# A two-stage vision block on one core: two roots to GpSimd as a power, 64x64 identity matmuls for the transposes, contiguous evictions, a new order with six early expert units

## The reference

```
x: (4, 64, 64, 16) fp32
x = x + conv_block(ln_over_channels(x))
t = tokens(x);  t = t + moe(ln(t));  x = from_tokens(t)

conv_block: x_dct = DCT over both axes
  low : 8x8 windows; q, k, v = window @ W; q, k normalised over the 64 places;
        attention over 16x16 channels per head; proj, bias
  high: h1 = gelu(1x1 conv); h1 = gelu(3x3 depthwise); x_conv = h1 + x_dct;
        h2 = gelu(1x1 conv of x_conv);  high = h2 + x_conv
  out = inverse DCT of (coef * low + (1 - coef) * high + x_dct)
moe: 8 experts 64 -> 256 -> 64 with exact gelu, all computed; the two largest
     router weights of a token gate the sum
```

## Time and profile before

| | us |
|---|---|
| Median of 3 runs (228.62 to 231.86) | 231.08 |
| The profiled execution | 230.22 |
| Its span, first to last instruction | 228.0 |
| PE busy | 199.9 (88%) |
| DVE busy | 131.4 (58%) |
| ACT busy | 127.3 (56%) |
| POOL busy | 51.9 (23%) |
| DMA, mean rate over the span | 63 GB/s |
| Mean granted TensorE clock | 0.978 |

### The profile page before, as it was taken

The page is one execution under the profiler, slowest core; times in us unless marked ns, Lnnn a source line. Parts: engine busy times, 40 slices in busy tenths (PEclk is TensorE's granted clock), DMA queues, the critical chain, the costliest instruction groups (busy, mean ns, idle before and its releaser), DMA issues.

```text
span 228.0 us, 6079 instructions
## 1 busy us (share of the span) xinstructions
PE 199.9 (88%) x2674; PEld 105.6 (46%) x2674; DVE 131.4 (58%) x231; ACT 127.3 (56%) x207; POOL 51.9 (23%) x54
## 2 busy tenths in 40 slices
PE   6868797999928977839689999999999999999992
PEld 2544486773404557737134344444444444444430
DVE  0597047909996998699981633554333554334554
ACT  2337942230072955546967587666687666786630
POOL 5380096019109996030120000000000000000000
PEclk9979999999997999997999999999999999999999
DMA  6990000000000000000004954360805406062001
GB/s 203 282 267 12 0 6 3 4 3 3 0 0 3 1 3 3 3 3 6 0 0 150 228 116 88 73 157 3 184 0 125 108 19 167 3 157 73 3 0 46
DMA packets 6601, 14.27 MB, mean 63 GB/s; under 512 B 2736, under 2 KB 4144, under 8 KB 5680
## 3 DMA queue, kind: packets, MB, share of 16 engines
q1 hardware_dynamic: 6576, 13.89, 24.8%
HBM read 12.71 MB, written 1.18 MB: 61 GB/s over the span
## 4 chain that ended last, share of the span: by engine, by line
PE 58%; DVE 26%; ACT 6%; DMA 5%; issue 3%; SPq 1%; DVEq 0%
PE psum L730 22%; PE psum L712 20%; PE psum L555 3%; DMA wide<-gate_store 2%; DMA xs<-in_x 2%; PE psum L529 2%; DVE place L1063 2%; PE psum L565 1%; PE psum L515 1%; DVE row L1062 1%; DVE place L1059 1%; DVE place L1007 1%; DVE place L1112 1%; DVE st L1106 1%; DVE st L1003 1%
## 5 line engine op out<-in xcount | busy, mean ns | idle before, releaser
L712 PE MATMUL psum<-tok,w1s 128*64 128x512 f16 x512 | 60.3, 382 | 2.0 <-ACT w1f L881 1.2
L1186 DVE SCALAR_TENSOR_TENSOR term<-psum,sm,wide 128x512 f32<-128x512 f32 x32 | 24.0, 751 | 59.1 <-PE psum L730 51.6
L881 ACT ACTIVATE hid<-psum,b1p 128x512 f32<-128x512 f32 x64 | 38.2, 700 | 15.5 <-PE psum L712 15.2
L712 PEld LDWEIGHTS psum<-tok,w1s 128*64 128x64 f16 x512 | 28.8, 111 | 35.5 <-issue 8.9
L730 PE MATMUL psum<-hid,w 128*64 128x512 f32 x128 | 28.9, 593 | 0.0
L881 ACT ACTIVATE w1f<-psum,b1p 128x512 f32<-128x512 f32 x32 | 19.5, 687 | 15.5 <-PE psum L712 15.4
L1191 DVE TENSOR_TENSOR x<-x,term 128x512 f32<-128x512 f32 x32 | 22.1, 692 | 1.1
L881 ACT ACTIVATE w1g<-psum,b1p 128x512 f32<-128x512 f32 x32 | 19.6, 712 | 0.3 <-PE psum L712 0.3
L730 PEld LDWEIGHTS psum<-hid,w 128*64 128x64 f32 x128 | 9.1, 137 | 15.0 <-issue 9.7
L555 PE MATMUL psum<-h_pad,tap_bd 64*64 64x512 f32 x144 | 16.0, 590 | 0.0
L730 PE MATMUL psum<-w1g,w 128*64 128x512 f32 x64 | 15.1, 594 | 0.1
(11 more groups left out here) (147 smaller groups left out, 289.9 us busy)
## 6 DMA issues: line engine op xcount, KB each, us to landing
wide<-gate_store SPq DMA_DIRECT2D x14, 512.0 KB, 6.3
xs<-in_x SPq DMA_DIRECT2D x2, 512.0 KB, 4.6
w1f<-in_W SPq DMA_DIRECT2D x2, 512.0 KB, 9.2
block_out<-x SPq DMA_DIRECT2D x4, 256.0 KB, 6.5
wide<-gate_store SPq DMA_DIRECT2D x2, 384.0 KB, 5.0
hid<-in_W1T SPq DMA_DIRECT2D x1, 512.0 KB, 10.2
w<-in_W SPq DMA_DIRECT2D x1, 512.0 KB, 12.3
sm<-in_small SPq DMA_DIRECT2D x1, 407.0 KB, 6.6
```

What stands on the lines that cost most here:

```text
L712: mm = pe.matmul(h_bank(tile)[side * H:(side + 1) * H, :], w1s[:, part, e, k * P + side * H:k * P + (side + 1) * H], tok[:, pair, half, b, :],
L881: act.activation(hid_of[u % 4][:, B2 * k + b, :], h_bank(tile), ACT.Gelu, bias=b1p[:, e * KT + k:e * KT + k + 1]).then_inc(gelu_ready, 1)
L1186: dve.scalar_tensor_tensor(term[:, u % 2, :], y_bank(u), b2t[:, e:e + 1], gate_b[part][:, e % (E // 2), :], ALU.add, ALU.mult).then_inc(te ...
```

## The change

- **Roots.** `inverse_root` stays for the column norms. For the norms of q and k and for the token variances, POOL does one `tensor_tensor` with the operation power and a tensor of -0.5 (new stages `root_of_norms`, `root_of_tokens`). DVE's stages are cut in two at that place (`inverse_norms` | `spread_roots`, `norm_tokens` | `scale_tokens`), with other work between.
- **Transposes.** `windows`, `places`, `heads` and `to_frequencies` become 32 matmuls of 64x64 blocks with a 64x64 identity each instead of 8 full transposes. Each has one semaphore increment at its end instead of one for each half.
- **Layout.** Copies from PSUM read and write in order (the output of `keep_dw` in runs of 8). The strides go into matmuls: `dct_over_w` and `windows` write PSUM with a step of 8 elements, `to_frequencies` loads weights with a step of 8, `inverse_over_kh` with a step of 16. `mix_branches` and `residual` lose their strides, the gates are made by one instruction instead of two, and the store of the gates writes 64-element runs.
- **Order.** All of `TURN` is new. Six units have an early `up` and two an early `down` and add. POOL makes the experts' weights (`weights_of_first`) after the first root.
- `SHARED` would give some of the copies to DVE; it is zero everywhere, so ACT does all of them.

```
 TURN = {
-    "router_weights": (1, 4), "keep_router_weights": (1, 4), "weights_of_first": (1, 2), "dct_over_h": (2, 3),
+    "root_of_norms": (1, 4), "root_of_tokens": (10, 12), "spread_roots": (9, 17), "scale_tokens": (30, 35),
+    "router_weights": (1, 4), "keep_router_weights": (3, 4), "weights_of_first": (2, 13), "dct_over_h": (2, 3),
...
-EARLY, EARLY_DOWN = 4, 0
-UPS = (45, 47, 48, 49, 50, 51, 52, 55)
-DOWNS = ()
-GELUS = (33, 34, 35, 36, 38, 39, 42, 44)
-ADDS = ()
+EARLY, EARLY_DOWN = 6, 2
+UPS = (45, 47, 48, 49, 50, 52, 54, 56, 58, 59, 60, 62)
+DOWNS = (53, 55)
+GELUS = (34, 35, 36, 37, 38, 40, 43, 44, 45, 46, 47, 50)
+ADDS = (39, 41)
...
-                    mm = pe.matmul(slot(p, 1)[rows_of(b), by_half(cp, side)], dh[p][rows_of(side), by_half(cp, b)], dct_w[rows_of(side)],
-                                   start=True, stop=True)
+                    to = bank(slot(p, 1), side).rearrange("p (m c) -> p c m", c=CP)[rows_of(b), cp]
+                    mm = pe.matmul(to, dh[p][rows_of(side), by_half(cp, b)], dct_w[rows_of(side)], start=True, stop=True)
...
-                for k2 in range(K):
-                    mm = pe.transpose(slot(p, 0)[:, k2 * P:(k2 + 1) * P], dw[p][:, k2 * P:(k2 + 1) * P], ident)
-                    if k2 % 4 == 3:
-                        mm.then_inc(xd_done, 1)
+                for k2, side, b in quarters():
+                    mm = pe.matmul(phase(slot(p, 0), b, k2)[rows_of(side)],
+                                      dw[p][rows_of(b), by_side(k2, side)], half_ident[rows_of(b)], start=True, stop=True)
+                mm.then_inc(xd_done, 1)
...
+                for k2, b, side in quarters():
+                    mm = pe.matmul(bank(slot(p, 1), side)[rows_of(b), k2 * H:(k2 + 1) * H],
+                                      phase(x_out[p], b, k2)[rows_of(side)], half_ident[rows_of(side)], start=True, stop=True)
+                mm.then_inc(back_done, 1)
...
+                of_channel = back[p].rearrange("p (m c) -> p c m", c=C)
...
-                    act.wait_ge(xd_done, 2 * p + j + 1)
-                    act.copy(xd[p].rearrange("p (n k) -> p k n", k=K)[:, 4 * j:4 * j + 4],
-                             bank(slot(p, 0), j).rearrange("p (k n) -> p k n", n=P)).then_inc(xd_ready, 1)
+                act.wait_ge(xd_done, p + 1)
+                for j in banks("xd", p):
+                    act.copy(bank(xd[p], j), bank(slot(p, 0), j)).then_inc(xd_ready, 1)
...
+            def root_of_norms(p):
+                pool.wait_ge(norms_read, p + 1)
+                r = root[:, p]
+                pool.tensor_tensor(r[:, 1, :], r[:, 3, :], minus_half[:, :], ALU.pow).then_inc(norm_roots, 1)
+
+            def root_of_tokens(p):
+                pool.wait_ge(vars_ready, p + 1)
+                two = lambda a: st[:, p, a:a + 2, :].rearrange("p a g -> p (a g)")
+                pool.tensor_tensor(two(4), two(2), minus_half[:, 0:2 * G], ALU.pow).then_inc(token_roots, 1)
```

More of the change, by code:

```diff
@@ L43 @@
 TURN = {
-    "router_weights": (1, 4), "keep_router_weights": (1, 4), "weights_of_first": (1, 2), "dct_over_h": (2, 3),
-    "square_columns": (2, 3), "dct_over_w": (5, 7), "windows": (6, 9), "conv_in": (8, 11), "keep_dw": (5, 7),
-    "keep_xd": (6, 9), "gelu_in": (8, 11), "norm_columns": (1, 2), "places": (10, 13), "keep_xt": (10, 12),
-    "join": (3, 5), "rest_ahead": (4, 7), "high": (6, 8), "gram_matrices": (12, 15), "gram_times_w": (14, 17),
-    "norms": (16, 20), "mask_gram": (5, 7), "taps": (19, 22), "logits": (18, 23), "products": (6, 9),
@@ L49 @@
-    "keep_tk": (13, 14), "inverse_norms": (8, 11), "scale_logits": (10, 14), "norms_of_k": (21, 25),
-    "softmax_in": (12, 15), "softmax_out": (13, 17), "gelu_depthwise": (15, 17), "gelu_out": (18, 22),
-    "conv_out": (24, 29), "project": (26, 31), "exponent": (16, 21), "heads": (27, 32), "times_wv": (28, 33),
-    "keep_y": (19, 23), "low": (30, 35), "mask_mix": (16, 19), "keep_yt": (20, 24), "to_frequencies": (34, 38),
-    "inverse_over_kh": (36, 41), "keep_back": (25, 27), "keep_half": (26, 29), "square_tokens": (28, 32),
@@ new lines @@
+    "square_columns": (1, 2), "dct_over_w": (5, 8), "windows": (6, 10), "conv_in": (7, 12), "keep_dw": (5, 8),
+    "keep_xd": (6, 10), "gelu_in": (7, 11), "norm_columns": (1, 2), "places": (9, 14), "keep_xt": (9, 13),
+    "join": (3, 6), "rest_ahead": (5, 8), "high": (7, 9), "gram_matrices": (11, 16), "gram_times_w": (13, 18),
+    "norms": (15, 20), "mask_gram": (4, 7), "taps": (19, 22), "logits": (17, 23), "products": (5, 8),
+    "keep_tk": (12, 14), "inverse_norms": (6, 11), "scale_logits": (12, 19), "norms_of_k": (21, 25),
@@ new lines @@
+    "softmax_in": (13, 20), "softmax_out": (14, 22), "gelu_depthwise": (15, 17), "gelu_out": (19, 22),
+    "conv_out": (26, 27), "project": (24, 30), "exponent": (16, 20), "heads": (28, 32), "times_wv": (29, 33),
+    "keep_y": (18, 23), "low": (31, 35), "mask_mix": (23, 25), "keep_yt": (21, 24), "to_frequencies": (34, 38),
+    "inverse_over_kh": (36, 40), "keep_back": (25, 27), "keep_half": (26, 29), "square_tokens": (28, 32),
+    "mix_branches": (24, 27), "inverse_over_kw": (37, 42), "high_part": (30, 42), "tokens": (39, 44),
@@ L114, in constants @@
     out[:, CONST["dct_h"]] = twice(centred.T)
-    out[:, CONST["dct_w"]] = twice(dct.T)
+    by_phase = np.arange(W).reshape(2, WW // 2, K).transpose(0, 2, 1).reshape(-1)
+    out[:, CONST["dct_w"]] = twice(dct.T[:, by_phase])
     out[:, CONST["idct_h"]] = twice(idct.T)
-    out[:, CONST["idct_w"]] = twice(idct.T)
+    out[:, CONST["idct_w"]] = twice(idct.T[by_phase])
     out[:, CONST["ident"]] = np.eye(P)
@@ L344, in metaformer @@
         norms_read = sem("norms_read")
+        norm_roots, vars_ready, token_roots = (sem(n) for n in ("norm_roots", "vars_ready", "token_roots"))
+        dw_other, xd_other, xt_other, yt_other, back_other, half_other = (
+            sem(f"{n}_other") for n in ("dw", "xd", "xt", "yt", "back", "half"))
         (sq_ready, dh_ready, dw_ready, xd_ready, h1_ready, halo_ready, xt_ready, gram_ready, prod_ready, tk_ready,
@@ L961, in weights_of_first @@
                 pool.tensor_tensor(w1s[:, 1, :, :], w1g[:, :, :], w1s[:, 0, :, :], ALU.subtract).then_inc(w1_ready, 1)
-            for stage, (p,) in in_turn((weights_of_first, join, rest_ahead, high, low_part)):
+            for stage, (p,) in in_turn((weights_of_first, join, rest_ahead, high, low_part, root_of_norms, root_of_tokens)):
                 stage(p)
@@ L1151, in shares @@
                 link(dve.scalar_tensor_tensor(L[5], L[5], 0.5, over(s[:, 14, :], E), ALU.mult, ALU.mult))
-                for half in range(2):
-                    part = lambda a: a[:, half * K:(half + 1) * K].rearrange("p (t b) e -> p b e t", b=B2)
-                    total = dve.scalar_tensor_tensor(gates[:, p, half], part(L[2]), 0.5, part(L[5]), ALU.mult, ALU.add)
-                total.then_inc(gparts_ready, 1)
+                by_row = lambda a: a.rearrange("p (t b) e -> p (b e) t", b=B2)
+                dve.scalar_tensor_tensor(gates[:, p].rearrange("p b e t -> p (b e) t"), by_row(L[2]), 0.5, by_row(L[5]),
+                                         ALU.mult, ALU.add).then_inc(gparts_ready, 1)
             def biases(p):
```

165 lines of the change are left out of this document (98 added, 67 removed).

## The result

The changed kernel takes 264.39 us (median of 3 runs, 264.13 to 264.93) against 231.08 us before: 1.148 times the time, 95% interval 1.137 to 1.159. It is 33.3 us slower, where 222.0 us was forecast. The profiled execution has a span of 262.6 us and a mean granted clock of 0.903 (before 228.0 and 0.978).

The account below looks back on a forecast made before the run. PE was taken to bound the rounds, no engine to be full in the front. Rounds begin at 119.3, plus 96.3 and 4.25 behind: 219.8 us span against 228.0, minus 8.2, so 222.0 us; range 216 to 230.

Parts of the forecast that it names:

- The price of the power: POOL's power for the roots: 3.1 us for 128x128, 0.8 for 128x32 with hand-over; ends 0.41 and about 10 us.
- 12%: Chance of the rival that POOL's power is long: gain used up at 6.4 us, 239 us in all at 10 us.
- The factor of 2: Each further us of a 128x128 power delays `norms_of_k` of pair 1 by 2, both pairs' powers sharing one POOL queue.
- the front: Work before the first `up`: `norms_of_k` of pair 1 at 63.5 us, first `up` at 99.9 us, a lead of 5.3.
- the early stretch: From first `up` to the rounds: twelve `up` and two `down`, paced by ACT, 19.4 us; rounds begin at 119.3 us.
- the sum of the softmax: Pair 0's softmax on DVE from 51.9 us: eleven steps, 7.6 us, plus some 2.6 us of holds by POOL; done at 62.1.
- The plan around the root: With the norms' root on POOL, pair 0's softmax starts at 51.9 us and `norms_of_k` of pair 1 at 63.5, 4.5 earlier.
- the break-even of 6.4 us: Length of a 128x128 power at which the gain of 8.2 us is used up, 3.1 + 8.2 / 2.5.
- fp32 matmuls lose nothing by strided reads: Read from L482's 1.14 us against L452's with columns in order; by it the strided PSUM writes were costed at nothing.
- The rule against this change: Strided PSUM writes in `dct_over_w` and `windows` slow matmuls; upper end twice the time, 4.6 us, costed at nothing.
- the rival of doubled writes: Strided PSUM writes cost twice: 222.0 + 4.6 = 226.6 us, no change that can be told; chance 10%.
- The rounds: PE-bound rounds of two `down` and two `up`, 6.88 us each; two units' `up` and `down` gone from them, leaving 96.3 us.

Follow-up runs that it names:

- the first runs: Changed kernel with both roots back on VectorE: 231.58 us with strided weights, 231.61 us with contiguous weights in `to_frequencies` and `inverse_over_kh`.
- the fastest kernel: Changed kernel with the norms' root as eleven ordinary POOL steps instead of one power, the tokens' root on VectorE: 226.96 us, in a second run 226.98 us.
- its early place: Both roots on VectorE, norms' root right behind the step reading the norms: 234.3 us (1.013) in the new order, 232.78 us (1.009) in the old up to the mix.
- the late place: Changed kernel with both roots on VectorE, as eight steps each where it waited for the power: 231.58 us, 1.003 of the kernel before.

## Why the prediction was wrong

- **The price of the power** is the step that failed: "I take 3.1 us for 128x128 ... and as ends 0.41 and about 10 us, three times the taken value, because nothing in the rows limits a function worked in software from above." It is 21.0 us, twice the upper end, and it alone makes the loss: with both roots on VectorE the kernel takes 1.003 of the time before, with eleven ordinary steps in the power's place 0.990. The sentence gives the reason not to name an upper end at all, and then names one. A case without any row above it should have had a larger chance than 12%, since the whole gain hung on it.
- **What a longer power costs** came out near the sum, in part by luck: 2.5 us for each us above 3.1 gives 222.0 + 2.5 x 17.9 = 266.8 for 21.0 us, measured 264.4. The factor of 2 held for the end of pair 1's power, 89.26 us instead of 54.7, 34.6 later. But by the forecast's own times nobody asks for that result before the softmax of pair 0 ends at 62.1, and this slack was not taken off: `norms_of_k` of pair 1 came 28.1 us later than forecast (91.63 against 63.5), not 35.8. With 2 x (5.43 - 0.8) = 9.3 us for the tokens' powers that makes 37.4 of the 42.4 us above 222.0. The other 5 were lost elsewhere, in the front and the early stretch, which took longer than forecast with a short root too (below). One reason was wrong: "DVE is held by POOL while it runs", which also stands in the sum of the softmax. VectorE's L1157 ran at its usual speed beside the power. VectorE was late because it waited for the result.
- **The plan around the root** was right at a small price. With POOL steps of 5.7 and 6.7 us, hidden as described, `norms_of_k` of pair 1 came at 62.55 us (63.5 forecast) and the kernel took 227.0 us. By the same slope and a length of 6.2 us it would have been 222.0 + 2.5 x 3.1 = 229.8: for want of the slack the break-even of 6.4 us was set too low.
- **"fp32 matmuls lose nothing by strided reads"** was read from L482, where the moving columns are strided, and I let it stand for weights too. For weights it is wrong: 201 to 214 against 134 ns a load, 0.9 us in each of four stages, which I did not cost. Against what it saved elsewhere it came to nothing in the first runs; in the old order contiguous weights in `to_frequencies` were 1.0 us better by the medians, within the intervals. The Trainium skill, SBUF — State Buffer, Door 1: The DMA port swizzle (why `[64,N]` ≈ `[32,N]`), has a note that SBUF is read in lines of 16 bytes and that a step beyond a line costs; the weight loads agree with it, the moving columns of L482 show no loss, though a loss of up to 0.3 us would be hidden there as in the stages above.
- **The rule against this change**, that any PSUM access that is not contiguous slows matmuls (the Trainium skill, PSUM — Partial Sum Buffer, Specifications (TRN2)), does not show in these stages: 1.16 us with a step of 32 bytes, 1.16 without. Costing them at nothing was right here, and the rival of doubled writes fell; a slowing too small to lengthen so short a stage is not ruled out.
- **The rounds** came out as worked: 96.3 forecast, 96.42 measured, and 96.55 in the fastest kernel. The early stretch, forecast at 19.4 us, took 20.5 there. The first `up`, forecast at 99.9, came at 103.66 there, 3.8 us late. Up to `times_wv` of pair 1 that run is within 0.2 us of the forecast's path (80.83 us, forecast 80.7); with the strided weights `inverse_over_kw` of pair 0 is 1.5 us late (88.85 against 87.4). The tokens' root, left on VectorE there, is 0.9 more. `tokens` of pair 1, forecast at 1.16, took 1.99 us (L682, at 101.74 in that run), another 0.8; about 0.6 I did not separate. The 1.99 us of before were read as a price of the stage, but they go with the clock: pair 0's stage took 1.16 us before, and the window of pair 1's has a granted clock of 0.50 (behind the five busy times):

```profile
103.28:105.20 1.92, 1.92 (x65) 1.80 (x65) 1.75 (x7) 1.01 (x1) 0.00 (x0) 0.50 0.00 0
```

- **The copies** came out as worked (0.59 us). So did the way from `heads` to `times_wv`, 1.16 + 1.2 in the forecast's path and 2.35 us in the run with the old order throughout, where it was 1.30: one increment at the end costs more than the "about 0.5 us" of the text above it.

What stays open: whether the new order as such is worth anything. With the root at its early place in both orders the intervals overlap, and the late place was run in the new order only.

## What to carry to other kernels

An operation with no row in any trace has no upper end; run it once by itself before an order is built on it, and let the forecast say so with a large chance on the far side. Moving a serial step to an idle engine pays if its result is ready before it is asked for: against the root on VectorE the same move lost 26 us with one instruction of 21 us and won 3 to 4.5 with eleven steps of 0.5 us (by the ratios to the kernel before on the same chip: 1.003 against 0.990 and 0.983). A stride does not vanish when a copy becomes contiguous: look where it went, and remember that TensorE's weights pay for it where its moving columns and its PSUM writes lost nothing that these short stages could show.
